# Single rows that land as two halves, 10 and 11 a group in place of 8 or 9 and 10

## The reference

```
w     = silu(ef1 @ rad_W1 + rad_b1) @ rad_W2 + rad_b2
      + silu(ef2 @ sph_W1 + sph_b1) @ sph_W2 + sph_b2        # one row of 128 for each edge
q, k, v = (x @ Wq)[dst], (x @ Wk)[src], (x @ Wv)[src]        # 8 heads of 16
alpha = sum over each head of (q * w * k) / sqrt(16) * edge_weight
out   = segment_sum(alpha * v, dst) / 16
y     = layernorm(x + out)
```

## Time and profile before

| | us |
|---|---|
| median of 3 runs (3109.12 to 3114.18) | 3112.95 |
| the profiled execution: its span, first to last instruction | 1968.8 |
| the profiled execution: its own time beside the span | not listed |
| median of the runs less that span | 1144.15 |
| busy in the span: PE | 1721.6 (87%) |
| busy: DVE | 1571.4 (80%) |
| busy: POOL | 1486.6 (76%) |
| busy: ACT | 580.1 (29%) |

### The profile page before, as it was taken

How to read it: one execution, slowest core, us unless ns; L and a number is a source line. 1 busy time by engine, 2 the same in 40 slices (tenths; PEclk the granted TensorE clock), 3 DMA queues, 4 the chain that set the end, 5 groups by cost and what they waited for, 6 DMA issues and landing times.

```text
span 1968.8 us, 57037 instructions
## 1 busy us (share of the span) xinstructions
PE 1721.6 (87%) x14511; PEld 1255.5 (64%) x14511; DVE 1571.4 (80%) x4327; ACT 580.1 (29%) x1031; POOL 1486.6 (76%) x1568
## 2 busy tenths in 40 slices
PE   8799999999998988888888888888888888888898
PEld 7566666666666666666666656666656565656666
DVE  5588888888887887787777878778777778777887
ACT  5332233333322322232222322222222222222223
POOL 7777777777777777777777777777777777777777
PEclk9899999999998999899888999899999989998988
DMA  9866656666666556555555555555556555565654
GB/s 340 257 173 173 176 173 175 174 175 169 168 169 172 162 167 174 153 172 163 166 154 171 164 166 170 156 173 155 173 156 172 161 166 167 162 172 156 174 154 116
DMA packets 191285, 339.03 MB, mean 172 GB/s; under 512 B 83101, under 2 KB 101262, under 8 KB 190958
## 3 DMA queue, kind: packets, MB, share of 16 engines
q0 software_dynamic: 74192, 202.08, 35.9%
q1 hardware_dynamic: 107696, 126.28, 21.6%
q10 hardware_dynamic: 9070, 7.02, 1.4%
HBM read 320.25 MB, written 14.95 MB: 170 GB/s over the span
## 4 chain that ended last, share of the span: by engine, by line
POOL 51%; PE 25%; issue 18%; DVE 3%; DMA 2%; DVEq 0%; ACT 0%; ACTq 0%; SPq 0%
POOL kvt L672 51%; PE bank L710 11%; PE bank L687 4%; PE bank L725 2%; PE bank L712 2%; DMA kvt<-kvtab,srcS 2%; PE bank L750 1%; PE bank L315 1%; PE bank L700 1%; DVE t L994 1%; PE bank L441 1%; DVE accT L948 1%; PE bank L429 1%; DMA qtab<-qx 0%; PE bank L419 0%
## 5 line engine op out<-in xcount | busy, mean ns | idle before, releaser
L672 POOL DMA_INDIRECT kvt<-kvtab,srcS x1527 | 1449.2, 949 | 465.9 <-issue 461.0
L796 ACT ACTIVATE hs<-bank,B 128x512 f32<-128x512 f32 x806 | 509.4, 683 | 1350.8 <-issue 783.4
L710 PE MATMUL bank<-W2r,hs 128*128 128x128 f32 x3224 | 494.8, 300 | 8.7 <-ACT hs L796 8.7
L994 DVE TENSOR_TENSOR t<-bank,kvt 128x512 f32<-128x512 f32 (+1 forms) x395 | 264.9, 671 | 292.8 <-DMA kvt<-kvtab,srcS 158.0
L710 PEld LDWEIGHTS bank<-W2r,hs 128*128 128x128 f32 x3224 | 419.2, 203 | 86.2 <-issue 71.8
L710 PE MATMUL bank<-W2s,hs 128*128 128x128 f32 x3224 | 453.3, 287 | 0.0
L710 PEld LDWEIGHTS bank<-W2s,hs 128*128 128x128 f32 x3224 | 421.3, 204 | 0.0
L725 PE MATMUL bank<-msg,oh 128*32 128x128 f32 x3216 | 177.4, 292 | 221.5 <-DVE accT L948 218.8
L725 PEld LDWEIGHTS bank<-msg,oh 128*32 128x32 f32 x3216 | 71.7, 109 | 411.8 <-issue 395.9
L1009 DVE TENSOR_REDUCE bank<-t 128x32 f32<-128x512 f32 x402 | 279.3, 695 | 13.8
L687 PE MATMUL bank<-eft,W 32*128 32x512 f32 x1612 | 279.2, 669 | 2.4 <-ACT kvh L481 2.4
(11 more groups left out here) (112 smaller groups left out, 704.5 us busy)
## 6 DMA issues: line engine op xcount, KB each, us to landing
kvA<-kvtab ACTq DMA_DIRECT2D x3968, 1.0 KB
kvS<-kvtab SPq DMA_DIRECT2D x3328, 1.0 KB
eft<-in_ef SPq DMA_DIRECT2D x102, 512.0 KB, 7.4
dbt<-dst SPq DMA_DIRECT2D x102, 384.0 KB, 6.7
kvt<-kvtab,srcS POOLq DMA_INDIRECT x1527
qwt<-qtab SPq DMA_DIRECT2D x403, 24.0 KB
kvtab<-kvt SPq DMA_DIRECT2D x24, 256.0 KB, 7.7
qtab<-qx SPq DMA_DIRECT2D x12, 384.0 KB, 6.4
```

What stands on the lines that cost most here:

```text
L672: pool.indirect_dma_start(kvt[:, (g - HX) % KS, t, :], None, kvtab, bass.IndirectOffsetOnAxis(ap=srcS[:, g * TG + t:g * TG + t + 1], axis= ...
L710: pe.matmul(WB[g % 2][:, t * D:(t + 1) * D], hs[:, g % HS, j, t * 128:(t + 1) * 128], w2[:, :], start=(j == 0 and t == 0), stop=False, ski ...
L796: act.activation(hs[:, g % HS, j, :], HB[i % 4][:, :], ACT.Silu, bias=B1[:, j:j + 1]).then_inc(m_si, 1)
L994: m = dve.tensor_tensor(t1[:, s, a:b, :], tiles(WB[s][:, :])[:, a:b, :], kv[:, :, 0:D], ALU.mult)
```

## The change

The two rates are raised: SP brings 10 rows in every group and ACT 11. The two buffers get a new shape: in place of one run of 256 floats for a row, each partition holds two pieces (`PIECES` = 2), first the K halves of both buffers and then the V halves. A row's transfer thus has a destination of two runs of 512 bytes, 1024 bytes apart, and its source is cut in the same way. VectorE's products for a row tile are written for the new shape, each over 8 heads of 16 of one half; there are still two instructions in place of one for such a group. Tables, registers and plans of groups follow from the rates at build time: 40 rows are loaded every four groups by SP and 22 (24 registers) every two by ACT; SP brings 31 tiles and ACT 34, where it was 26 and 31.

```diff
-RS, RA = (8, 9, 272), (10, 10, 0)
+RS, RA = (10, 10, 0), (11, 11, 0)
+PIECES = 2
...
-        kvS = sb("kvS", [128, 2, 2 * D], f32)
-        kvA = sb("kvA", [128, 2, 2 * D], f32)
+        kvS = sb("kvS", [128, PIECES, 2, 2 * D // PIECES], f32)
+        kvA = sb("kvA", [128, PIECES, 2, 2 * D // PIECES], f32)
...
             def kv_row(reg):
-                return kv_bytes[bass.ds(start_of(reg, (N - 1) * KVROW), KVROW)].rearrange("(o f) -> o f", o=1)
+                return kv_bytes[bass.ds(start_of(reg, (N - 1) * KVROW), KVROW)].rearrange("(o a f) -> o a f", o=1, a=PIECES)
...
-                        sp.dma_start(kvS[p:p + 1, u % 2, :].bitcast(u8), kv_row(sp_row[r - rows_upto(g // BS * BS, RS)])
+                        sp.dma_start(kvS[p:p + 1, :, u % 2, :].bitcast(u8), kv_row(sp_row[r - rows_upto(g // BS * BS, RS)])
...
-                        act.dma_start(kvA[p:p + 1, u % 2, :].bitcast(u8), kv_row(act_row[r - rows_upto(g // BA * BA, RA)])
+                        act.dma_start(kvA[p:p + 1, :, u % 2, :].bitcast(u8), kv_row(act_row[r - rows_upto(g // BA * BA, RA)])
...
-            def kv_parts(g):
-                rows = kv_rows(g)
-                if g in use_s:
-                    return (0, KT, rows[:, 0:KT, :]), (KT, TG, kvS[:, use_s[g] % 2:use_s[g] % 2 + 1, :])
-                if g in use_a:
-                    return (0, KT, rows[:, 0:KT, :]), (KT, TG, kvA[:, use_a[g] % 2:use_a[g] % 2 + 1, :])
-                return ((0, TG, rows),)
+            def heads(t):
+                return t.rearrange("p (h d) -> p h d", h=H)
+
+            def row_tile(g, k):
+                buffer, u = (kvS, use_s[g] % 2) if g in use_s else (kvA, use_a[g] % 2)
+                half = buffer[:, k * PIECES // 2:(k + 1) * PIECES // 2, u, :]
+                return half if PIECES == 2 * H else half.rearrange("p a (h d) -> p (a h) d", d=HD)
...
-                for a, b, kv in kv_parts(g):
-                    m = dve.tensor_tensor(t1[:, s, a:b, :], tiles(WB[s][:, :])[:, a:b, :], kv[:, :, 0:D], ALU.mult)
+                n = gathered(g)
+                m = dve.tensor_tensor(t1[:, s, 0:n, :], tiles(WB[s][:, :])[:, 0:n, :], kv_rows(g)[:, 0:n, 0:D], ALU.mult)
+                if n == KT:
+                    m = dve.tensor_tensor(heads(t1[:, s, KT, :]), heads(tiles(WB[s][:, :])[:, KT, :]), row_tile(g, 0),
+                                          ALU.mult)
```

More of the change, by code:

```diff
@@ L1025, in gnn_program @@
                 dve.wait_ge(m_al, g + 1)
[L1026 to L1030, removed]
+                m = dve.tensor_tensor(msg[:, g % MS, 0:n, :].rearrange("p t (h d) -> p t h d", h=H),
+                                      kv_rows(g)[:, 0:n, D:2 * D].rearrange("p t (h d) -> p t h d", h=H),
+                                      cut_alpha(g)[:, 0:n * H].rearrange("p (t h a) -> p t h a", h=H, a=1)
+                                      .broadcast_to([128, n, H, HD]), ALU.mult)
+                if n == KT:
+                    m = dve.tensor_tensor(heads(msg[:, g % MS, KT, :]), row_tile(g, 1),
+                                          cut_alpha(g)[:, KT * H:TG * H].rearrange("p (h a) -> p h a", a=1)
+                                          .broadcast_to([128, H, HD]), ALU.mult)
                 m.then_inc(m_msg, 1)
```

## The result

The changed kernel takes 4636.33 us (median of four runs, 4623.22 to 4645.01); the kernel before took 3113.56 in the same comparison. The ratio is 1.4897, 95% interval 1.4857 to 1.4937. The forecast was 3210 within 3100 to 3268: the sign was right, and the size wrong by a factor of nearly sixteen (+97 against +1523).

What follows compares the result with a forecast made beforehand. It took POOL's gathers to bound the kernel before and SP's queue the changed one: 77.6 us of excess instructions plus 23.8 for halves less 4.5 gave +97, so 3112.95 + 97 = 3210 us, range 3100 to 3268.

Steps and rivals of the forecast that it cites:

- The price of two halves: Row transfers on SP and ACT: +6 ns for each two-piece row, 23.8 us on SP for 3968 rows.
- the sum: SP's queue: 77.6 us of excess instructions plus 23.8 for halves less 4.5, +97 us; POOL's gain not added.
- Rival C: Row transfers: two pieces cost 79 ns more than one, as ten do; much slower, 3500 us; chance 0.08.
- Against the execution's own time: Whole run: 1144.15 us between profiled span and median time carried over unchanged, so 3112.95 + 97 = 3210 us.
- rival B: SP's queue: saving just falls short, or runs have more room on SP; no difference, 3113 us; chance 0.08.
- What it adds on SP: SP's queue: 640 more rows and more register loads, 257.9 us against 180.3 us of waits, 77.6 too much.
- What the change takes from POOL: POOL's gathers: 1519 in place of 1527, eight fewer, 10.0 us saved while POOL stays the bound.
- The order of effects on SP: SP's in-order queue: its excess delays query fetches, then TensorE and VectorE; POOL fills its buffers and waits; +97 us.
- the mark: Sign of a right forecast, at POOL: it waits some 100 us for VectorE's messages.
- the other marks: Profile signs: row median 230 to 240 ns (over 290 wrong), query fetches 4.9 us apart, span near 2066 us.
- ACT: it becomes full, hardly longer than POOL's pace: ACT's queue: 203 us of added work against about 205 us free, lying beside SP's longer work.
- The page of the skill that was set against the row: SP's row issue: by its rule 640 rows cost next to nothing, leaving POOL's 10 us; forecast countered with 0.32 us each.

Runs made afterwards that it cites:

- e5: Changed kernel at the old rates (SP 8 or 9, ACT 10 rows), a row's two halves landing in two partitions; 3081.74 us, ratio 0.9994.
- e6: Changed kernel at the old rates, a row landing as 16 pieces of 64 bytes in one partition; 3664.0 us, ratio 1.1899.
- e1: The kernel before, unchanged, run and profiled again; 3105.6 us, ratio 1.0001, profiled span 3105.1 us.
- e2: The kernel before with only the rates raised to 10 and 11, rows in one piece; 3102.77 us, ratio 0.9991.
- e7: Changed kernel at the old rates, two halves on SP only, ACT's rows in one piece; 3429.71 us, ratio 1.1139.
- e3: Changed kernel with the two halves alone, at the old rates (SP 8 or 9, ACT 10 rows); 4202.03 us, ratio 1.3528.
- e12: The kernel before, with POOL gathering for the first 15 groups only; 1920.91 us, ratio 0.6175.
- e13: The changed kernel, with POOL gathering for the first 15 groups only; 3852.57 us, ratio 1.2384.
- e4: The kernel before without single rows on SP or ACT, POOL gathering those tiles instead; 2756.93 us, ratio 0.8875.
- e11: The kernel before without rows on SP and with 3 rows a group on ACT; 2839.99 us, ratio 0.9139.
- run 228: Not a follow-up run: "one run" means a row landing as one contiguous piece; its median issue time is 228 ns on SP, 235 on ACT.

## Why the prediction was wrong, step by step

**"The price of two halves": the step that failed.** It took +6 ns, from the biases' transfer of three pieces, and named +79 ns, from ten pieces, as the upper end. Measured: 563 − 228 = +335 ns on SP, +335 on ACT. On SP alone 3968 × 0.335 is 1329 us where the sum had 23.8. The mistake was to rank transfers by their number of pieces. By e5 the +6 was right, +9 measured, for pieces in different partitions, and those were the only rows that the earlier trace rows offered; by e6 the number is nearly irrelevant. A row cut inside one partition had none in the trace. The nearest in form, line 397's at 423 ns, was in the trace but not in the earlier trace rows; by it the upper end would have been +195 ns and not +79, and even that would not have held +335.

**Rival C** (two pieces take the way that ten take) had the right kind of cause, but 79 ns and 3500 us; its chance of 0.08 and its place outside the range came from the same ranking.

**"Against the execution's own time": wrong as well.** The 1144.15 us were carried over as lying around the span; e1 shows that they lie within it, as stalls. The profiled execution was a different one in kind, not an execution of the runs with something around it. The doubt stood in rival B only ("more room on SP"), at 0.08.

**"What it adds on SP": the terms were right in the main and the room wrong.** The added instructions went out nearly as computed (199 loads in place of 202), but the runs had 563 us of room in place of 180.3, so that e2 comes out at 0.9991. This overcharge of 77.6 us is small beside the other error and has its opposite sign.

**"What the change takes from POOL": no gain, and the sum was right to leave it out.** But POOL is not the bound in the runs, as the earlier trace rows had it: it waits 1106.5 us for messages in e1, and eight gathers fewer save nothing.

**The order of effects on SP was right, the right sign partly luck.** SP becomes the bound, its waits leave the loop, POOL fills its buffers and waits for VectorE, the query fetches move apart. But the start was another one: in e1 POOL already waits 1106.5 us for messages, 2232.4 after, where the mark had some 100. The median over 290 ns, the fetches at 11.2 us against 4.9 and the span of 4642.8 against 2066 are the other marks that went wrong. And with the room of the runs the sum's own 257.9 + 23.8 us would have been hidden on SP, and the kernel would have come out even, as rival B has it. That it came out slower is owed to the price that the prediction had too low.

**"ACT: it becomes full, hardly longer than POOL's pace": too mild.** Its rows rose by 335 ns too; e7 against e3 shows that these are worth about 750 us, more than SP's.

**The page of the skill that was set against the row** (the Trainium skill, "DMA: Bandwidth & Descriptors", section "Issuing engines are not separate DMA queues": the time to initiate a DMA is usually small beside the DMA itself). How long a row's transfer itself takes, no row of these traces tells; but the issue is not negligible, and less so than the prediction said: at 0.56 us for a row of 1024 bytes, SP's row line is 56% of the chain.

**The sum, made again.** e2 and the changed kernel issue the same 3968 rows on SP. From the first row to the last SP's queue takes 2916 us in e2 and 4474 in the changed kernel. Added up over the queue, the rows with their MOVE and the idle time behind each take 2098 and 3702 us of it, 0.53 and 0.93 us a row; all else, waits included, takes 818 and 772. So the loss stands in the rows: 1329 us by the medians, and some 275 more because rows are stretched further than in e2. With hardly a gather a row takes 0.34 us (e12) and 0.72 (e13). ACT's queue is as full: its rows take 4043 of 4447 us.

**What stays open.** What holds up SP, ACT and the starts on VectorE while POOL gathers; why the profiled execution of 1968.8 us, with all its gathers, has none of this; and why ten rows on ACT alone cost as much as rows on both queues. The runs show that the stalls need the gathers (e12) and grow with rows beside them (e4, e11, e1). They show neither that mechanism nor what in the form of a row costs the 335 ns.

## To carry to other kernels

Price a transfer by a row of exactly its form, in which partitions and dimensions its pieces lie, and not by its number of pieces; where the trace has no such row, the upper bound is open, and a short kernel with that one transfer is worth more than any argument. Before a sum is made on a profile, hold its span against the timed runs: at 1969 against 3113 us it is a profile of something else, and which engine sets the end in it says little about the runs. If pieces must lie apart, different partitions cost 9 ns a row here and one partition 335.

## What the runs showed of the hardware that was not expected

- Issue time of a 1024-byte row, its address in a register, by form, median on SP and ACT: one run 228 and 235 ns; two runs in two partitions 237 and 243; two runs in one partition 563 and 570; sixteen runs in one partition 538 and 542.
- In the timed runs POOL's gathers slow the other queues down: 3105 us with gathers and rows, 2757 with gathers alone (e4), 1921 with rows and hardly a gather (e12), while a gather's median stays at 946 ns (e1, e4, e12). A row on SP takes 0.57 us in the mean with gathers and 0.34 with hardly one. In a stall eight rows that SP issues in 2.48 us take 5.41, and a product starts 5.6 us after the matmul it waited for.
- TensorE's mean granted clock goes with it, as a share of its upper level of 2.4 GHz: 0.967 in e12, where TensorE is busy for 89% of the span, 0.769 in e1 (65%), 0.657 in the changed kernel (52%). TensorE's busy time for the same 14511 matmuls is 1716.1, 2009.2 and 2420.3 us. This makes the chain longer where TensorE stands in it, but is not the cause of the change's loss: in the chain of the changed kernel TensorE has 2%.
